# Two-layer graph kernel on one core: the last pass's row statistics and norms shared out anew, adjacency turned by halves, two fetches and one copy at other places

## The chip, the cores and the metric

The kernel runs on 1 core of one Trainium2 chip. The metric is the device time of one execution in microseconds (us). Engines are called PE (TensorE), ACT (ScalarE), DVE (VectorE), POOL (GpSimd) and SP (SyncE, which here only issues DMAs).

## The reference

Eight batches, each with x (1024 rows of 512) and a sparse adj (1024 x 1024). Cut to what matters:

```
x = layernorm(x + L0(x, adj))
x = layernorm(x + L1(x, adj))

L0: w = exp(-0.5 * (adj - mean_k)^2 / (1e-14 + precision_k^2))   for 4 kernels k
    w = w / sum_k w;  ws_k = row sum of w_k
    out[:, k-th 128 columns] = ws_k * x @ W_k.T
L1: top1 = argmax(mean over rows of x @ router_w + router_b)       one of 4 experts per batch
    out = adj @ (x @ expert_w[top1])
    y = relu(batchnorm of out over all batches of one expert)
```

## The kernel before

A tile is 128 rows of one batch: 64 tiles, 8 per batch. Products are made of fp16 halves (high and low part, three products for one). One loop of steps n runs over the tiles on every engine; the engines keep in step by semaphores alone, and each engine's order is as written.

**Main loop, step n.** SP loads adj tile n+2 (L342) and x tile n+3 (L350), turns adj tile n+1 (L362, a transposing DMA from `adj_cut` into `adjT`) and x tile n+2 (L369), stores finished pairs of x1 rows (L459) and L1 units (L487). POOL scales and splits adj tile n+1 (L526 to L531) and x tile n+2 (L538, L540), squares a part (L546, L549), and in odd steps norms two finished tiles (`norm_pair`, L556 to L575). `adj_in` is a ring of 3 tiles. ACT makes squares and exponentials of tile n (L677, L683, L689) and the reciprocal of the sum for tile n-1 as Ln and Exp (L693, L695); DVE adds the four weights up in `ps_t` (L1000), makes weighted row sums (L962), adds the product to x (L984) and takes statistics (L933, L939). PE multiplies x by W (L1156, bank `ps_h`), then the L1 units.

**L1 units.** L1 is computed in the order adj @ x first, then times the expert. A z unit u (8 per batch) is a 128 x 512 block of the transposed adj @ x: 24 matmuls into one of two `ps_z` banks (L1170). ACT copies its high part to `zT` (`take_z`, L705), DVE its low part (`low_z`, L927). PE may start unit u only when the low part of unit u-2 is done. Units 0 to 3 of a batch use the first half of adj's rows, 4 to 7 the second. Unit n-9 is made in step n; step 11 alone makes two, 1 and 2. Four z units later, o unit u multiplies `zT` by the batch's expert `w_sel` (L1188) in step u+13. The expert is picked by a small chain on DVE that ends in `hot_row` (L921) in step 8m+12 for batch m; SP waits for it (L475), and then fetches 1 MB to `w_sel` (L476) in step 8m+13, ahead of that step's turned tiles.

**`adjT`** is double-buffered by batch, laid out as (batch parity, high or low, tile, row): both halves of the rows lie mixed, so its space comes free only when all 8 z units of the batch are done.

**After the loop** come the remaining z and o units on PE, then the batchnorm constants, and the last pass over n = 0 to 7 (batches 7, 6, 0, 1, ..., 5). For each n: L1 output `o` and x1 come back from DRAM into space that the main loop left (`fetch_o`, `fetch_x1`); `affine` applies the constants (ACT L781, POOL L637 for n = 2 and 5); PE transposes each 128 x 512 row tile back (L1237); DVE adds relu of it to x1 (L1110 plain, L1113 with a row sum). "Even" rows get their statistics on DVE (bn_stats L1088, bn_aggr L1096), the others, "odd" rows, get their row sum with the addition and their squares on ACT (L790). ACT turns both into 1/std (L810, L813), and POOL norms the 8 row tiles (L629); for n = 6 ACT norms the last four (L796), with mean times 1/std from POOL (L623). SP stores y in halves of 1 MB (L417), the last one in two pieces (L409, L411).

Even rows are every second one, and all of the last four. ACT's written order in the last pass (L850 ff.) is: half of `affine(n+1)`, `odd_squares(n-2, 1)`, `inverse_std(n-2)`, the other half, `odd_squares(n-1, 0)`.

Of the kernel before, what the change touches and what calls it, by code (L numbers as in the profile page):

```python
# [12 lines left out]
P = 128  # L13
# [39 lines left out]
def gnn_program(nc, x, adj, mean_rel, prec_rel, w0, router_w, router_b, expert_w, gamma, beta, x1_spill,  # L53
# [15 lines left out]
    with ExitStack() as ctx:  # L69
# [11 lines left out]
        adjT = sb("adjT", [P, 2, 2, T, NR], F16)  # L81
# [99 lines left out]
        adjT_flat = flat(adjT[:], "a h t n").bitcast(F32)  # L181
# [52 lines left out]
        early_in = flat(adjT[:, 1], "h t n").bitcast(F32).rearrange("p (e n) -> p e n", e=E)  # L234
# [26 lines left out]

        def even_rows(j):

            return (j + 1) // 2 if j <= END_ROWS else END_ROWS // 2 + j - END_ROWS

        def is_even(j):
            return j % 2 == 0 or j >= END_ROWS
# [66 lines left out]
        def _(sp):  # L334
# [17 lines left out]
            def turn_adj(m):  # L352

                b, t = m // T, m % T
                if m == T:
                    sp.wait_ge(dve_wlo, 2 * (E - 1))
                if t == 0:
                    wait(sp, pe_z, (b - 2) * T + G)
                if t == G:
                    wait(sp, pe_z, (b - 2) * T + T)  # L360
                sp.wait_ge(pool_al, m + 1)
                sp.dma_start_transpose(adjT[:, b % 2, :, :, t * P:(t + 1) * P].rearrange("p h t n -> p (h t) n"),  # L362
                                       flat(adj_cut[:, m % 2], "h n")).then_inc(adj_turned[m % 2], 16)
# [12 lines left out]
            def fetch_o(n):  # L376
# [7 lines left out]
                elif 1 < n < NB:  # L384
                    if n == 2:
                        sp.wait_ge(pe_h, TILES)
                    elif n == 3:
                        sp.wait_ge(pe_z, TILES - T)
                    elif n == 4:
                        sp.wait_ge(pe_z, TILES)  # L390
                    elif n == 5:
                        sp.wait_ge(pe_o, TILES)
# [8 lines left out]
                    for h in range(2):  # L401
                        sp.dma_start(o_buf[i][h], o_lines[b, h]).then_inc(o_back[i], 16)

            def store_y(n):
                for g in range(2):
                    dst = rows_of(out, n)[g]
                    if n == NB - 1 and g == 1:
                        sp.wait_ge(dve_out, G // 2)
                        sp.dma_start(dst[:, 0:G // 2], y_buf[n][g][:, 0:G // 2]).then_inc(y_stored[n % RING], 16)  # L409
                        sp.wait_ge(act_out, G + G // 2)  # L410
                        sp.dma_start(dst[:, G // 2:G], y_buf[n][g][:, G // 2:G]).then_inc(y_stored[n % RING], 16)  # L411
                        continue
                    if n == NB - 2 and g == 1:
                        sp.wait_ge(act_out, G)
                    else:
                        sp.wait_ge(pool_out, n * T + (g + 1) * G - (G if n == NB - 1 else 0))
# [36 lines left out]
            for n in range(LAST):  # L453
# [10 lines left out]
                if u % T == 0 and 0 <= u < TILES:  # L464
                    m = u // T
# [6 lines left out]
                    wait(sp, pe_o, u)  # L472
                    if u == 0:
                        sp.wait_ge(planes_stored, 16 * E)
# [24 lines left out]
            for n in range(4, RING):  # L499
                fetch_o(n)  # L500
                fetch_x1(n)
# [14 lines left out]
        def _(pool):  # L516
# [93 lines left out]
            def minus_mean(n, first, last):  # L610

                at, even, odd = n % 4, slice(first, last, 2), slice(first + 1, last, 2)
                pool.wait_ge(dve_mv2, even_rows(n * T + last))
                g.tensor_scalar(r_neg[:, at, even], r_mv[:, at, even, 0], -1.0, 1.0, ALU.mult, ALU.mult).then_inc(pool_small, 1)
                pool.wait_ge(dve_y2, n * T + last)
                g.tensor_scalar(r_neg[:, at, odd], r_mv[:, at, odd, 0], -1.0 / D, 1.0, ALU.mult, ALU.mult).then_inc(pool_small, 1)
# [29 lines left out]
            for n in range(NB):  # L646
# [20 lines left out]
        def _(act):  # L667
# [29 lines left out]
            def take_z(n):  # L697
                for u in z_unit(n):
# [25 lines left out]
            for n in range(LAST):  # L724
# [16 lines left out]
                if z_taken_first(n - 1):  # L741
                    take_z(n - 1)
                take_o(n - 1)
                if not z_taken_first(n - 1):
                    take_z(n - 1)
# [38 lines left out]
            def odd_squares(n, h):  # L784

                for t in (h * G + 1, h * G + 3):
                    k = n * G + t // 2
# [10 lines left out]

            lns = [0]

            def inverse_std(n, first, last):

                at = n % 4
                groups = [(slice(first, last), 1.0)]
                if n * T + last <= END_ROWS:
                    groups = [(slice(first, last, 2), 1.0), (slice(first + 1, last, 2), float(D) ** -3)]
                    act.wait_ge(act_ssq, n * G + last // 2)
                act.wait_ge(dve_mv2, even_rows(n * T + last))
                for rows, scale in groups:
                    s.activation(r_lnv[:, at, rows], r_mv[:, at, rows, 1], ACT.Ln, bias=eps_out, scale=scale).then_inc(act_lnv, 1)  # L810
# [8 lines left out]
            for n in range(2, NB + 1):  # L819
# [18 lines left out]
        def _(dve):  # L838
# [290 lines left out]
        def _(pe):  # L1129
# [30 lines left out]
            def z_product(u):  # L1160
# [5 lines left out]
                for t in range(T):  # L1166
                    if u % T == 0:
                        pe.wait_ge(pool_1l, u + t + 1)
                    for i, (left, right) in enumerate(PRODUCTS):
                        last = te.matmul(ps_z[:, u % 2, :], x1p[:, b % 2, left, t, k * P:(k + 1) * P],  # L1170
                                         adjT[:, b % 2, right, t, half * HALF:(half + 1) * HALF],
# [95 lines left out]
```

## Time and profile before

| | us |
|---|---|
| median of 3 runs | 880.13 |
| lowest to highest | 879.94 to 881.65 |
| profiled execution, its own time | 878.73 |
| span in the profile | 876.9 |
| PE, DVE, ACT, POOL busy | 754.6, 754.9, 756.3, 704.8 |

The profile divides one execution into instructions with start and duration. "Idle before <-X" is how long the engine stood still before an instruction, and whose semaphore ended it. The main loop runs to about 710 us, PE alone goes on to 797 us, and the last pass fills the rest.

### The profile page before, as it was taken

Reading aid. Unit: us, or ns where it says so; the run is one execution under the profiler, and the core shown is the slowest. Engines: PE = TensorE matmul, PEld = TensorE weight load, DVE = VectorE, ACT = ScalarE, POOL = GpSimd, SP = SyncE. Lnnn points to the kernel's source line nnn. Section 1 sums busy time; section 2 is a strip of 40 time slices with the busy share of each in tenths; the row PEclk is TensorE's granted clock in tenths of the full one; section 3 lists DMA queues with packets and bytes.
Section 4 is the critical chain, followed back from the end, with each engine's and each line's share of the span. In section 5 each row is a group of like instructions: output and inputs, shape, how many; then the busy total and the mean of one; then the engine's idle time right before and its main releaser. Section 6 shows DMA issues by size and latency. Waiting matters only on the chain.

```text
span 876.9 us, 12591 instructions
## 1 busy us (share of the span) xinstructions
PE 754.6 (86%) x3922; PEld 356.6 (41%) x3922; DVE 754.9 (86%) x1643; ACT 756.3 (86%) x774; POOL 704.8 (80%) x808
## 2 busy tenths in 40 slices
PE   1444469899999999999999999999999999997772
PEld 1111124344444444444444444444444444444561
DVE  2999988999999999999999999999999992226995
ACT  6999998999999999999999999999999961115983
POOL 6599989899999999999999999999999732003795
PEclk9766669999999999999999999999999999998996
DMA  8899998988797779888987797779887828219999
GB/s 231 209 278 260 213 238 190 217 195 193 193 240 193 193 193 240 193 193 193 239 195 193 193 241 192 193 187 242 197 193 168 158 81 339 96 67 397 342 388 390
DMA packets 251254, 191.72 MB, mean 219 GB/s; under 512 B 210098, under 2 KB 210098, under 8 KB 245170
## 3 DMA queue, kind: packets, MB, share of 16 engines
q1 hardware_dynamic: 251042, 190.90, 81.3%
q8 instruction: 31, 0.51, 0.3%
q14 instruction: 37, 0.30, 0.1%
q10 hardware_dynamic: 144, 0.00, 0.0%
HBM read 91.78 MB, written 48.76 MB: 160 GB/s over the span
## 4 chain that ended last, share of the span: by engine, by line
POOL 35%; DVE 28%; PE 15%; ACT 13%; issue 6%; DMA 2%; SPq 1%; POOLq 0%; DVEq 0%; ACTq 0%
DVE ps_t L1000 12%; DVE wgt L962 11%; PE ps_z L1170 8%; POOL adj_cut L531 7%; POOL x_turn L540 4%; POOL adj_cut L529 4%; POOL adj_in L526 3%; POOL x1p L575 3%; PE ps_o L1188 3%; ACT ps_t L689 3%; ACT ps_t L695 3%; ACT ps_t L693 3%; DVE x_in L984 2%; POOL x_in L566 2%; POOL x_turn L538 2%
## 5 line engine op out<-in xcount | busy, mean ns | idle before, releaser
L1170 PE MATMUL ps_z<-adjT,x1p 128*128 128x512 f16 x1536 | 342.3, 379 | 0.6 <-POOL x1p L575 0.6
L1156 PE MATMUL ps_h<-w0T,x_turn 128*128 128x512 f16 x768 | 194.5, 407 | 74.2 <-DVE x_in L984 63.0
L1000 DVE TENSOR_TENSOR ps_t<-ps_t,wgt 128x1024 f32<-128x1024 f32 x192 | 235.4, 1226 | 16.6 <-ACT ps_t L689 11.7
L962 DVE SCALAR_TENSOR_TENSOR wgt<-wgt,ps_t 128x1024 f32<-128x1024 f32 x192 | 224.7, 1215 | 16.4 <-ACT ps_t L695 16.4
L1170 PEld LDWEIGHTS ps_z<-adjT,x1p 128*128 128x128 f16 x1536 | 150.1, 98 | 182.5 <-POOL x1p L575 2.5
L677 ACT ACTIVATE wgt<-adj_in,neg_mu 128x1024 f32<-128x1024 f32 x192 | 205.7, 1135 | 7.3 <-POOL neg_mu L593 7.3
L683 ACT ACTIVATE wgt<-wgt 128x3072 f32<-128x3072 f32 x64 | 176.5, 2758 | 0.0
L1188 PE MATMUL ps_o<-zT,w_sel 128*128 128x512 f16 x696 | 159.7, 379 | 1.7 <-DMA w_sel<-w_planes 0.9
L1156 PEld LDWEIGHTS ps_h<-w0T,x_turn 128*128 128x128 f16 x768 | 74.9, 103 | 182.4 <-issue 103.2
L531 POOL TENSOR_TENSOR adj_cut<-adj_in,adj_cut 128x1024 f16<-128x1024 f32 x64 | 138.3, 2160 | 5.3
L1188 PEld LDWEIGHTS ps_o<-zT,w_sel 128*128 128x128 f16 x696 | 68.0, 98 | 84.2 <-DMA w_sel<-w_planes 1.4
L984 DVE SCALAR_TENSOR_TENSOR x_in<-ps_h,wsum,x_in 128x128 f32<-128x128 f32 x256 | 82.8, 345 | 8.8
L927 DVE SCALAR_TENSOR_TENSOR zT<-ps_z,zT 128x512 f16<-128x512 f32 x64 | 43.3, 676 | 47.7 <-ACT zT L705 47.7
L526 POOL TENSOR_SCALAR adj_in<-adj_in 128x1024 f32<-128x1024 f32 x63 | 66.8, 1061 | 17.0 <-DMA adj_in<-in_adj_dram 12.1
L575 POOL TENSOR_TENSOR x1p<-x_in,x1p 128x512 f16<-128x512 f32 x64 | 75.3, 1177 | 5.3
L540 POOL TENSOR_TENSOR x_turn<-x_in,x_turn 128x512 f16<-128x512 f32 x64 | 74.3, 1161 | 5.3
L689 ACT ACTIVATE ps_t<-adj_in 128x1024 f32<-128x1024 f32 x64 | 65.8, 1028 | 11.0 <-DVE wgt L962 8.7
L529 POOL TENSOR_SCALAR adj_cut<-adj_in 128x1024 f16<-128x1024 f32 x64 | 69.0, 1077 | 5.2
L705 ACT ACTIVATE zT<-ps_z 128x512 f16<-128x512 f32 x64 | 37.3, 584 | 40.1 <-PE ps_z L1170 40.1
L693 ACT ACTIVATE ps_t<-ps_t 128x1024 f32<-128x1024 f32 x64 | 64.6, 1009 | 5.7 <-DVE ps_t L1000 3.5
L695 ACT ACTIVATE ps_t<-ps_t 128x1024 f32<-128x1024 f32 x64 | 64.5, 1008 | 2.0
L677 ACT ACTIVATE adj_in<-adj_in,neg_mu 128x768 f32<-128x768 f32 (+1 forms) x64 | 62.1, 970 | 0.0
(222 smaller groups left out, 810.2 us busy)
## 6 DMA issues: line engine op xcount, KB each, us to landing
adj_in<-in_adj_dram SPq DMA_DIRECT2D x64, 512.0 KB, 4.3
x_in<-in_x_dram SPq DMA_DIRECT2D x64, 256.0 KB, 4.4
x_spill<-x_in SPq DMA_DIRECT2D x28, 512.0 KB, 3.4
out_spill<-o_stage SPq DMA_DIRECT2D x50, 256.0 KB, 3.5
w_sel<-w_planes SPq DMA_DIRECT2D x8, 1024.0 KB, 7.8
adjT<-x_spill SPq DMA_DIRECT2D x6, 1024.0 KB, 8.6
out_dram<-adjT SPq DMA_DIRECT2D x5, 1024.0 KB, 6.3
adjT<-out_spill SPq DMA_DIRECT2D x4, 1024.0 KB, 12.6
```

The costliest lines, as they stand in the source:

```text
L529: g.tensor_scalar(cut[:, 0, :], tile, 1.0, 1.0, ALU.mult, ALU.mult).then_inc(pool_ah, 1)
L531: g.tensor_tensor(cut[:, 1, :], tile, cut[:, 0, :], ALU.subtract).then_inc(pool_al, 1)
L540: g.tensor_tensor(cut[:, 1, :], tile, cut[:, 0, :], ALU.subtract).then_inc(pool_xl, 1)
L575: g.tensor_tensor(x1p[:, b % 2, 1, t, :], row, x1p[:, b % 2, 0, t, :], ALU.subtract).then_inc(pool_1l, 1)
L677: s.activation(to, adj_in[:, n % ADJ_RING, first:NR], ACT.Square, bias=neg_mu[:, k:k + 1], scale=spread[k]).then_inc(act_sq, 1)
L683: s.activation(w, w, ACT.Exp, scale=-1.0).then_inc(act_w, 1)
L962: v.scalar_tensor_tensor(out=wgt[:, m % 2, j, :], in0=wgt[:, m % 2, j, :], scalar=SUM_SCALE / W0_SCALE, in1=tot, op0=ALU.mult, op1=ALU.mul ...
L984: last = v.scalar_tensor_tensor(out=row[:, f], in0=ps_h[:, m % 2, f], scalar=wsum[:, m % 2, COLUMN[k]:COLUMN[k] + 1], in1=row[:, f], op0=A ...
L1000: v.tensor_tensor(tot, tot, wgt[:, n % 2, j, :], ALU.add).then_inc(dve_tot, 1)
L1156: last = te.matmul(ps_h[:, n % 2, :], xT[:, n % 2, left, c, :], w0T[:, right, c, :], start=(c + i == 0), stop=(c == C - 1 and i == 2))
L1170: last = te.matmul(ps_z[:, u % 2, :], x1p[:, b % 2, left, t, k * P:(k + 1) * P], adjT[:, b % 2, right, t, half * HALF:(half + 1) * HALF], ...
L1188: last = te.matmul(ps_out(u), w_sel[:, left, c, k * P:(k + 1) * P], zT[:, right, half, c, :], start=(c + i == 0), stop=(c == C - 1 and i = ...
```

## The change

1. **Rows of n = 5 and 6** (`few`): one row tile in four is even (was one in two). The squares of four more row tiles go from DVE's bn_stats to ACT.
2. **Norms of n = 5**: as for n = 6, POOL norms four row tiles and ACT the last four (`norm_late`). ACT's norms of n = 5 stand after `odd_squares(6, 0)`.
3. **`adjT` by halves**: laid out as (batch parity, half, high or low, tile, row within the half). Parts 4 and 5 of the buffer, the place of `o` for n = 4, are now the first half of the last batch, and come free after z unit 59 instead of 63. `fetch_o(4)` moves into `fetch_x1(3)`; the first half of `fetch_o(5)` waits for z unit 63 instead of the last o unit.
4. **Expert's fetch**: in step 8m+12 instead of 8m+13, ahead of that step's turned tiles.
5. **Z unit 2**: ACT's copy goes behind `weigh_others(12)`, DVE's low part from step 12 to the start of step 13.

```diff
-        adjT = sb("adjT", [P, 2, 2, T, NR], F16)
+        adjT = sb("adjT", [P, 2, 2, 2, T, HALF], F16)
...
+        def few(n):
+            return n in (5, 6)
+        def is_even(j):
+            return j % (4 if few(j // T) else 2) == 0 or j >= END_ROWS
...
+        def z_halves(n):
+            return z_unit(n)[:1], z_unit(n)[1:]
...
                     elif n == 4:
+                        sp.wait_ge(pe_z, TILES - G)
+                    elif n == 5:
                         sp.wait_ge(pe_z, TILES)
-                    elif n == 5:
-                        sp.wait_ge(pe_o, TILES)
...
                     for h in range(2):
+                        if n == 5 and h == 1:
+                            sp.wait_ge(pe_o, TILES)
                         sp.dma_start(o_buf[i][h], o_lines[b, h]).then_inc(o_back[i], 16)
...
                     if n == 3 and g == 1:
+                        fetch_o(4)
                         sp.wait_ge(pe_z, TILES)
...
-                if u % T == 0 and 0 <= u < TILES:
-                    m = u // T
+                if (u + 1) % T == 0 and 0 <= u + 1 < TILES:
+                    m = (u + 1) // T
...
                     sp.wait_ge(dve_route, m + 1)
-                    wait(sp, pe_o, u)
+                    wait(sp, pe_o, u + 1)
...
-                    if n == NB - 2:
+                    if few(n):
                         minus_mean_over_std(n, G, T)
-                    norm_rows(n, range(0, G if n == NB - 2 else T))
+                    norm_rows(n, range(0, G if few(n) else T))
...
                     weigh_others(n)
+                    take_z(z_halves(n - 1)[1])
...
                 if n == NB:
-                    act.wait_ge(pool_nmr, 1)
-                    norm(NB - 2, range(G, T))
+                    norm_late(NB - 2)
                 odd_squares(n - 1, 0)
+                if n == NB - 1:
+                    norm_late(NB - 3)
...
-                    for u in z_unit(n - 1):
+                    for u in (*z_halves(n - 2)[1], *z_halves(n - 1)[0]):
                         low_z(u)
```

How the instructions stand before and after, at three places. The lines of the changed kernel have other numbers; the operations are the same.

ACT from the z copies of step 12 on, before (L705 copies a z unit, L693 and L695 make the reciprocal, L683 the exponentials, L677 the squares):

```order
L705 ACTIVATE zT<-ps_z 128x512 x2
L693 ACTIVATE ps_t<-ps_t 128x1024
L695 ACTIVATE ps_t<-ps_t 128x1024
L683 ACTIVATE wgt<-wgt 128x3072
L677 ACTIVATE adj_in<-adj_in,neg_mu 128x1024
L689 ACTIVATE ps_t<-adj_in 128x1024
```

The same place in the changed kernel:

```order
L727 ACTIVATE zT<-ps_z 128x512
L715 ACTIVATE ps_t<-ps_t 128x1024
L717 ACTIVATE ps_t<-ps_t 128x1024
L705 ACTIVATE wgt<-wgt 128x3072
L727 ACTIVATE zT<-ps_z 128x512
L699 ACTIVATE adj_in<-adj_in,neg_mu 128x1024
L711 ACTIVATE ps_t<-adj_in 128x1024
```

The second copy, of unit 2, now stands behind the reciprocal and the exponentials.

SP in steps 20 and 21, before (the row of `w_sel` is the fetch of batch 1's expert, TENSOR_LOAD the read of its number):

```order
L362 DMA_TRANSPOSE adjT<-adj_cut 128x16x128
L487 DMA out_spill<-o_stage 128x512
L369 DMA_TRANSPOSE x_turn<-x_turn 128x8x128
L342 DMA adj_in<-in_adj_dram 128x1024
L350 DMA x_in<-in_x_dram 128x512
L475 TENSOR_LOAD sc_int
L475 ISA x2
L476 ISA
L476 DMA w_sel<-w_planes 128x4096
L362 DMA_TRANSPOSE adjT<-adj_cut 128x16x128
```

In the changed kernel:

```order
L494 TENSOR_LOAD sc_int
L494 ISA x2
L495 ISA
L495 DMA w_sel<-w_planes 128x4096
L378 DMA_TRANSPOSE adjT<-adj_cut 128x16x128
L506 DMA out_spill<-o_stage 128x512
L385 DMA_TRANSPOSE x_turn<-x_turn 128x8x128
L358 DMA adj_in<-in_adj_dram 128x1024
L366 DMA x_in<-in_x_dram 128x512
L378 DMA_TRANSPOSE adjT<-adj_cut 128x16x128
```

The wait for the expert's number and the fetch moved ahead of a turned adj tile, a store, a turned x tile and the loads of adj tile 23 and x tile 24.

ACT in the last pass, before, from the squares of n = 5 (in `zT`) on; n = 6 lies in `x_turn` and `w0T`, n = 7 in `adjT`:

```order
L790 ACTIVATE ps_z,adj_in<-zT,adj_in 128x512 x4
L810 ACTIVATE adj_in<-adj_in,eps 128x4 x2
L813 ACTIVATE adj_in<-adj_in 128x8
L790 ACTIVATE ps_z,adj_in<-x_turn,adj_in 128x512 x2
L790 ACTIVATE ps_z,adj_in<-w0T,adj_in 128x512 x2
L810 ACTIVATE adj_in<-adj_in,eps 128x4 x2
L813 ACTIVATE adj_in<-adj_in 128x8
L796 ACTIVATE w0T<-w0T,adj_in 128x512 x4
L790 ACTIVATE ps_z,adj_in<-adjT,adj_in 128x512 x2
```

In the changed kernel:

```order
L815 ACTIVATE ps_z,adj_in<-zT,adj_in 128x512 x6
L841 ACTIVATE adj_in<-adj_in,eps 128x2
L841 ACTIVATE adj_in<-adj_in,eps 128x2x3
L844 ACTIVATE adj_in<-adj_in 128x8
L815 ACTIVATE ps_z,adj_in<-x_turn,adj_in 128x512 x3
L821 ACTIVATE zT<-zT,adj_in 128x512 x4
L815 ACTIVATE ps_z,adj_in<-w0T,adj_in 128x512 x3
L841 ACTIVATE adj_in<-adj_in,eps 128x2
L841 ACTIVATE adj_in<-adj_in,eps 128x2x3
L844 ACTIVATE adj_in<-adj_in 128x8
L821 ACTIVATE w0T<-w0T,adj_in 128x512 x4
L815 ACTIVATE ps_z,adj_in<-adjT,adj_in 128x512 x2
```

ACT has four more squares and four more norms here, and the norms of n = 5 stand between the two groups of squares of n = 6.

## Rows read from the trace of the kernel before

**Rows 1.** Waits from 160 to 720 us: total us, times, longest us

```profile
POOL adj_in L546 <- ACT wgt L677: 6.6, 1, 6.6
ACT ps_t L689 <- POOL adj_in L549: 1.8, 7, 0.3
PE ps_o L1188 <- DMA w_sel<-w_planes: 0.9, 1, 0.9
```

**Rows 2.** Timeline of ACT, step 12: start us, duration us, operation, idle before

```profile
146.55 0.60 ACT L705 ACTIVATE zT<-ps_z 128x512 f16<-128x512 f32 x1 [2.21 <-PE ps_z L1170]
147.04 1.02 ACT L693 ACTIVATE ps_t<-ps_t 128x1024 f32<-128x1024 f32 x1
```

**Rows 3.** Timeline of DVE, steps 12 and 13

```profile
143.60 1.23 DVE L1000 TENSOR_TENSOR ps_t<-ps_t,wgt 128x1024 f32<-128x1024 f32 x1
...
154.02 1.22 DVE L1000 TENSOR_TENSOR ps_t<-ps_t,wgt 128x1024 f32<-128x1024 f32 x1
...
158.53 0.67 DVE L927 SCALAR_TENSOR_TENSOR zT<-ps_z,zT 128x512 f16<-128x512 f32 x1
159.13 0.17 DVE L939 BATCH_NORM_AGGREGATE y_mv<-y_stat 128x2 f32<-128x6 f32 x1
```

**Rows 4.** Timeline of POOL, steps 13 and 22

```profile
159.46 0.19 POOL L556 TENSOR_SCALAR rstd<-y_mv 128x2 f32<-128x2 f32 x1 [3.04 <-DVE y_mv L939]
...
253.80 1.05 POOL L526 TENSOR_SCALAR adj_in<-adj_in 128x1024 f32<-128x1024 f32 x1
```

**Rows 5.** Timeline of DVE, step 20: the expert's number is ready

```profile
241.15 0.20 DVE L921 TENSOR_SCALAR hot_row<-ps_s,sc_idx 1x4 f32<-1x4 f32 x1
```

**Rows 6.** Timeline of SP's queue, steps 21 and 22

```profile
242.85 0.35 SPq L476 DMA_DIRECT2D w_sel<-w_planes  x1
243.89 6.42 SPq L362 DMA_TRANSPOSE adjT<-adj_cut  x1
...
253.00 0.48 SPq L342 DMA_DIRECT2D adj_in<-in_adj_dram  x1
```

**Rows 7.** DMA issues of the whole page: count, KB each, median us to landing

```profile
adj_in<-in_adj_dram SPq DMA_DIRECT2D x64, 512.0 KB, 4.3
...
w_sel<-w_planes SPq DMA_DIRECT2D x8, 1024.0 KB, 7.8
```

**Rows 8.** DMA issues from 752 to 760 us alone, same columns

```profile
w_sel<-w_planes SPq DMA_DIRECT2D x1, 1024.0 KB, 4.8
```

**Rows 9.** Windows: busy us of PE, PEld, DVE, ACT, POOL; clock, DMA share, GB/s

```profile
765.00:775.00 10.00, 10.00 (x48) 4.51 (x46) 5.29 (x25) 1.79 (x3) 0.00 (x0) 1.00 0.00 1
...
846.00:862.00 16.00, 11.29 (x64) 8.94 (x64) 16.00 (x53) 9.24 (x26) 15.71 (x28) 0.99 1.01 402
```

**Rows 10.** Timeline of DVE, last pass, n = 7

```profile
857.97 0.69 DVE L1088 BATCH_NORM_STATS2 y_stat<-adjT 128x6 f32<-128x512 f32 x1
858.57 0.67 DVE L1110 SCALAR_TENSOR_TENSOR adjT<-ps_h,adjT 128x512 f32<-128x512 f32 x1
```

**Rows 11.** Timeline of ACT, last pass, n = 5 to 7

```profile
846.01 0.67 ACT L790 ACTIVATE ps_z<-zT,adj_in 128x512 f32<-128x512 f32 x1
...
846.72 0.67 ACT L790 ACTIVATE ps_z<-zT,adj_in 128x512 f32<-128x512 f32 x1
...
850.56 0.21 ACT L813 ACTIVATE adj_in<-adj_in 128x8 f32<-128x8 f32 x1
...
858.09 0.21 ACT L813 ACTIVATE adj_in<-adj_in 128x8 f32<-128x8 f32 x1
860.36 2.93 ACT L796 ACTIVATE w0T<-w0T,adj_in 128x512 f32<-128x512 f32 x4 [2.07 <-POOL adj_in L623]
...
864.51 0.18 ACT L790 ACTIVATION_READ_ACCUMULATOR ps_z<-adjT,adj_in 128x1 f32 x1
...
865.25 0.21 ACT L813 ACTIVATE adj_in<-adj_in 128x4 f32<-128x4 f32 x1
```

**Rows 12.** Timeline of POOL, last pass, n = 5 to 7

```profile
853.67 6.05 POOL L629 TENSOR_SCALAR zT<-zT,adj_in 128x512 f32<-128x512 f32 x8
...
860.12 0.20 POOL L623 TENSOR_TENSOR adj_in<-adj_in 128x4 f32<-128x4 f32 x1
860.31 3.03 POOL L629 TENSOR_SCALAR x_turn<-x_turn,adj_in 128x512 f32<-128x512 f32 x4
...
865.63 3.47 POOL L629 TENSOR_SCALAR adjT<-adjT,adj_in 128x512 f32<-128x512 f32 x4 [1.97 <-ACT adj_in L813]
```

**Rows 13.** Timeline of SP's queue: the first of the last three stores

```profile
869.12 0.33 SPq L417 DMA_DIRECT2D out_dram<-adjT  x1
```

More of the change, by code:

```diff
@@ L180, in gnn_program @@
         wgt_flat = flat(wgt[:], "a k n")
-        adjT_flat = flat(adjT[:], "a h t n").bitcast(F32)
+        adjT_flat = flat(adjT[:], "a g h t n").bitcast(F32)
         x1p_flat = flat(x1p[:], "a h t n").bitcast(F32)
@@ L260, in gnn_program, with of_rows @@
         END_ROWS = NB * T - G
+        def few(n):
+            return n in (5, 6)
+        def is_even(j):
+            return j % (4 if few(j // T) else 2) == 0 or j >= END_ROWS
         def even_rows(j):
-            return (j + 1) // 2 if j <= END_ROWS else END_ROWS // 2 + j - END_ROWS
-        def is_even(j):
-            return j % 2 == 0 or j >= END_ROWS
+            return sum(is_even(i) for i in range(j))
+        def of_rows(x, n, first, last, odd):
+            if not few(n):
+                return x[:, slice(first + odd, last, 2)]
+            lines = x[:, first:last].rearrange("p (h t) -> p h t", t=G)
+            return lines[:, :, slice(1, G) if odd else slice(0, 1)]
         BY_POOL = (2, 5)
@@ L498, in _ @@
             fetch_x1(3)
-            for n in range(4, RING):
-                fetch_o(n)
-                fetch_x1(n)
+            fetch_x1(4)
+            fetch_o(5)
+            fetch_x1(5)
             fetch_o(6)
@@ L695, in sum_reciprocal, with take_z @@
                 s.activation(tot, tot, ACT.Exp, scale=-1.0).then_inc(act_rec, 1)
-            def take_z(n):
-                for u in z_unit(n):
+            def take_z(units):
+                for u in units:
                     half, k = u % T // G, u % G
@@ L784, in odd_squares @@
             def odd_squares(n, h):
-                for t in (h * G + 1, h * G + 3):
-                    k = n * G + t // 2
+                for t in range(h * G, (h + 1) * G):
+                    if is_even(n * T + t):
+                        continue
+                    k = n * T + t - even_rows(n * T + t)
                     act.wait_ge(dve_y2, n * T + t + 1)
@@ L797, in norm, with norm_late @@
                                  scale=r_std[:, n % 4, t:t + 1]).then_inc(act_out, 1)
+            def norm_late(n):
+                act.wait_ge(pool_nmr, sum(few(m) for m in range(n + 1)))
+                norm(n, range(G, T))
             lns = [0]
@@ L803, in inverse_std @@
                 at = n % 4
-                groups = [(slice(first, last), 1.0)]
+                lnv, square = r_lnv[:, at], r_mv[:, at, :, 1]
+                groups = [(lnv[:, first:last], square[:, first:last], 1.0)]
                 if n * T + last <= END_ROWS:
-                    groups = [(slice(first, last, 2), 1.0), (slice(first + 1, last, 2), float(D) ** -3)]
-                    act.wait_ge(act_ssq, n * G + last // 2)
+                    groups = [(of_rows(lnv, n, first, last, odd), of_rows(square, n, first, last, odd), scale)
+                              for odd, scale in ((0, 1.0), (1, float(D) ** -3))]
+                    act.wait_ge(act_ssq, n * T + last - even_rows(n * T + last))
                 act.wait_ge(dve_mv2, even_rows(n * T + last))
-                for rows, scale in groups:
-                    s.activation(r_lnv[:, at, rows], r_mv[:, at, rows, 1], ACT.Ln, bias=eps_out, scale=scale).then_inc(act_lnv, 1)
+                for to, of, scale in groups:
+                    s.activation(to, of, ACT.Ln, bias=eps_out, scale=scale).then_inc(act_lnv, 1)
                 lns[0] += len(groups)
@@ L1170, in z_product @@
                         last = te.matmul(ps_z[:, u % 2, :], x1p[:, b % 2, left, t, k * P:(k + 1) * P],
-                                         adjT[:, b % 2, right, t, half * HALF:(half + 1) * HALF],
+                                         adjT[:, b % 2, half, right, t, :],
                                          start=(t + i == 0), stop=(t == T - 1 and i == 2))
```

27 lines of the change are left out of this document (15 added, 12 removed).

## The prediction

> **What bounds the kernel now.** I read the waits of the main loop first, then the timelines of ACT, DVE and POOL where a wait stands out, then the last pass by windows and by each engine's timeline.
>
> Main loop: from 160 to 720 us POOL waits for nothing worth naming but once for 6.6 us, at the very end where it has no more tiles [rows 1]. An engine that never waits sets the pace. ACT and DVE form a ring of nearly the same length: ACT waits for POOL's square seven times, 1.8 us in all [rows 1]. So whatever lets POOL start its unbroken run earlier moves the whole loop and, behind it, the products that PE makes alone up to 797 us. That run starts at 159.46, after a wait of 3.04 us for DVE's statistics [rows 4].
>
> Last pass: DVE is busy 16.00 of 16 us and POOL 15.71, while DMA stands at 1.01 of its share and ACT works only 9.24 [rows 9]. Three resources are full at once; ACT has the room. The end goes by POOL: it norms n = 5 from 853.67, hands out L623 at 860.12 [rows 12], ACT, which had 1/std ready at 858.30 and stood idle 2.07 us, norms its rows till 863.3, then squares rows of n = 7 and gives 1/std at 865.46 [rows 11]; POOL norms four rows from 865.63 to 869.10, and SP's first store of the last three goes out at 869.12 [rows 12, 13].
>
> **Z unit 2's copy (step 12).** ACT waits 2.21 us for PE before it copies unit 2, and the reciprocal behind it starts at 147.04 [rows 2]. Without that copy it needs only DVE's sum, which ends at 143.60 + 1.23 = 144.83 [rows 3]: start 144.87, 2.17 us earlier. The copy comes back behind the exponentials, where unit 2 is long done, and takes about 0.5 us of ACT (0.60 less the overlap of two neighbours: 146.55 to 147.04 [rows 2]). So the sum that DVE starts at 154.02 [rows 3] starts 1.7 us earlier, and from there the ACT and DVE ring is 1.7 us ahead. In step 13 DVE has one more low part before its statistics, 0.60 us (158.53 to 159.13 [rows 3]); they come 1.7 - 0.6 = 1.1 us earlier, and so does POOL's start at 159.46 [rows 4]. The ring's extra 0.6 us is lost, since it waits for POOL after some steps.
>
> One item adds to this. PE waits once for `w_sel`, 0.9 us [rows 1]; ACT then falls back some 0.5 us behind POOL and stays there. With a fetch that lands earlier this goes. So the loop ends between 1.1 (POOL's shift alone) and 1.7 us (all of the ring's) earlier; I take 1.5.
>
> **The expert's fetch.** For m = 1 the number is ready at 241.15 + 0.20 = 241.35 [rows 5], and SP issues the fetch at 242.85 [rows 6], held up by two loads ahead of it. Now SP stands waiting, and issues at about 242.1. What is queued behind it counts: turned tile 21, a store, turned x tile 22, then the load of adj tile 23, which POOL wants at 253.80 [rows 4]. In the trace the turned tile behind the fetch holds SP for 6.42 us [rows 6]: its end, 250.31, is 0.3 us before the fetch lands by the median of 7.8 us. A fetch with nothing ahead of it in the queues lands in 4.8 us [rows 8]. By that: 242.1 + 4.8 - 0.3 = 246.6 for the turned tile. From the end of the turned tile to the adj load are 253.00 - 250.31 = 2.7 us [rows 6], of which a store of x1 (0.6) now falls behind it: load at 248.7, landed 4.3 us later [rows 7] at 253.0. POOL wants it at 253.80, in later batches some 0.6 us later against the number, once ACT and DVE run right behind POOL. Margin 0.8 to 1.4 us: cost nothing. With the median 7.8 us it is the first rival. Turned x tile 22 is issued at about 247.4 and wanted by PE only after 255.
>
> The Trainium skill (DMA: Bandwidth & Descriptors, Anatomy of one DMA) gives 2.0 us plus bytes over 436 GB/s, for another way of issuing: 4.4 us for 1 MB, near the 4.8 that the trace has for a fetch alone, against the 7.8 with loads ahead of it. By it the margin would be 0.4 us wider and the sum the same.
>
> **adjT by halves, fetches of the last pass.** DMA stands still in 765 to 775 us (share 0.00 [rows 9]), so 2 MB of n = 4 move from the crowded time after 784 to the idle time after 755. PE reads the same 512 columns in one piece as before, and the transposing DMA writes pieces of the same 128 columns at another distance: I cost that at nothing, between plus and minus 1 us. At 1 MB in 2.5 us (425 GB/s) the move frees 4.9 us of DMA. But no engine of the last pass waits for a fetch now; the gain comes at the end alone, where the stores of n = 6 still run when those of n = 7 are issued at 869.12. The last 2 MB need 4.9 us in any case, and the end at 876.9 leaves 7.8 us from the issue; a start at once and a late completion take some 7.3. So 0.3 to 0.8 us, I take 0.5.
>
> **Statistics and norms.** DVE loses four bn_stats, 0.60 us each (857.97 to 858.57 [rows 10]), and four aggregates of about 0.1: 2.7 us, and the rows of n = 7 are ready 2.7 us earlier. This does not reach the end, because ACT now becomes the bound. ACT, in times of the old trace: six squares of n = 5, 0.71 apart (846.01 to 846.72 [rows 11]), till 850.3; 1/std ready at 851.1 (before 850.77); three squares of n = 6 till 853.2. POOL ends n = 4 and hands out L623 for n = 5 at 853.8, by the same 0.45 us that it takes behind n = 5 [rows 12]. ACT norms four rows, 4 x 0.71, till 856.7; three more squares till 858.9; 1/std of n = 6 at 859.7, where it was 858.30. POOL, with four rows less, has waited since 857 and gives L623 at 860.0 (before 860.32). ACT's norms end at 862.9, two squares at 864.4 (before 864.69), 1/std at 865.15 (before 865.46). POOL's last four rows and the store move by the same 0.3 us. So of DVE's 2.7 us and POOL's 3 us, 0.3 are left. Bounds: 0.3 later if each of the eight more ACT operations costs 0.1 more, 2.7 earlier if ACT were no bound.
>
> **Sum.** 1.5 + 0.5 + 0.3 = 2.3 us. The profiled execution took 878.73 (span 876.9): 876.4. Its time lies 1.4 below the median of 880.13, so the median becomes **877.8**.
>
> **Rivals.**
> 1. *The fetch holds SP, and POOL runs dry.* If the fetch takes 7.8 us [rows 7] with nothing ahead of it, the turned tile ends at 249.6, adj tile 23 lands at 256.0, and POOL, which has no slack, waits 1.5 to 2.2 us after each of seven fetches: 10 to 15 us. The point from which it decides is a landing of about 6 us. For it: the four queued items are all ahead of the load now. Against it: the 4.8 us row. Net 880.1 - 2.3 + 12 = 889, slower by 1%.
> 2. *ACT is no bound in the last pass* (it fits its new work into its idle time): DVE's 2.7 us count, and the freed DMA time lets them: 880.1 - 1.5 - 0.5 - 2.7 = 875.4. Against it: ACT's list above has no idle stretch longer than 0.6 us between 846 and 857.
> 3. *The main loop gives nothing back*: PE or a DMA takes the place of the wait at 146.55. PE has to make units 3 and 4 in the same order, and unit 4 needs unit 2's low part just when PE is ready for it (157.5 against 157.9). Then only the last pass's 0.8 us are left: 879.3, within 0.2%. The same holds if the turned halves or ACT's new work cost as much as they give.
>
> **How the numbers follow.** Forecast 0.52, rival 3 and its kin 0.24, rival 2 0.12, rival 1 0.12. A measurement of this kernel can tell some 0.2% from no change, 1.76 us: faster means below 878.4, slower above 881.9. The forecast, with main loop 1.1 to 1.7, end 0.3 to 0.8, statistics -0.3 to 0.6, runs from 877.0 to 879.0; about a tenth of its chance lies in "same". Faster 0.6, same 0.28, slower 0.12. The range leaves out rival 1 and little else: 875.0 to 881.0.
>
> **What would show it.** Step 12: no wait of ACT before unit 2's copy, POOL's L556 of step 13 about 1.1 us earlier. Main loop: POOL without waits at tile 8m+15, ACT waiting for L549 oftener than seven times. From 755 us a fetch of 2 MB. Last pass: ACT full from 846 to 864, POOL idle some 2.5 us between its norms of n = 5 and n = 6, DVE waiting or ending early; last stores issued about 1.8 us earlier. Wrong would be: waits of POOL for `adj_in` with the fetch ahead (rival 1), or POOL's last norms 2 us or more earlier than 0.3 against 797 us (rival 2).

## The result, and the profile after

| | before | after |
|---|---|---|
| median, us | 880.17 (879.49 to 881.78, 8 runs) | **883.67** (883.3 to 885.45, 8 runs) |
| profiled execution, its own time | 878.73 | 883.32 |
| span in the profile | 876.9 | 881.5 |

The ratio is 1.0038, 95% interval 1.0028 to 1.0047: slower by 0.4%. Forecast were 877.8 us and a range of 875.0 to 881.0. On another chip, in the experiments below, the same kernel came to 885.06 us against 879.91 (1.0057, 1.0043 to 1.0071).

The waits of after from 160 to 720 us (total us, times, longest us) answer to [rows 1]:

```profile
ACT ps_t L711 <- POOL adj_in L568: 10.6, 24, 1.6
...
POOL adj_in L565 <- ACT wgt L699: 5.9, 1, 5.9
POOL adj_in L545 <- DMA adj_in<-in_adj_dram: 5.6, 8, 1.4
```

The last row is new. POOL, which sets the pace of the loop and had not waited for an adj tile, now waits for one after each of the first seven fetches of an expert (the eighth has no adj tile behind it). ACT, one step behind in the ring, hands this on: 10.6 us in 24 waits where it had 1.8 in 7. PE's one wait for `w_sel` [rows 1] is gone, as meant.

SP's own waits of after over the same stretch, same columns, say what it stands for (L50 is the helper that waits on a semaphore, here for PE's o unit 8m-1; L494 reads the expert's number):

```profile
SPq L50 <- PE ps_o L1220: 39.1, 6, 7.6
SPq L494 <- DVE hot_row L953: 16.1, 6, 2.7
```

That is 55 us in six fetches, 9 us each. Before, SP waited for neither of the two. Most of the time, 39.1 us, goes to o unit 8m-1, which still reads the old expert in `w_sel`; the expert's number ends the last 2.7 us. About half of the 9 us SP would have stood in any case: before, it stood until 236.33 (below) for POOL's part of tile 21. The other half is new, and while SP stands, nothing else is issued. In the window of 238 to 242 us (columns as in [rows 9]; the first line is before, the second after) DMA was full, and is empty now:

```profile
238.00:242.00 4.00, 4.00 (x20) 1.85 (x19) 3.87 (x14) 3.71 (x4) 3.67 (x6) 1.00 1.10 234
```

```profile
238.00:242.00 4.00, 4.00 (x20) 1.80 (x19) 3.87 (x13) 3.70 (x5) 3.67 (x5) 1.00 0.00 0
```

SP's queue before, steps 20 and 21, which goes on in [rows 6] (start us, us that SP is held, operation):

```profile
236.33 1.48 SPq L362 DMA_TRANSPOSE adjT<-adj_cut  x1
...
241.20 0.33 SPq L342 DMA_DIRECT2D adj_in<-in_adj_dram  x1
```

The same of after, steps 20 to 22, behind DVE's line that gives the expert's number (ready at 240.39):

```profile
240.19 0.20 DVE L953 TENSOR_SCALAR hot_row<-ps_s,sc_idx 1x4 f32<-1x4 f32 x1
```

```profile
241.16 0.35 SPq L495 DMA_DIRECT2D w_sel<-w_planes  x1
241.56 5.26 SPq L378 DMA_TRANSPOSE adjT<-adj_cut  x1
246.87 0.57 SPq L506 DMA_DIRECT2D out_spill<-o_stage  x1
247.55 1.29 SPq L385 DMA_TRANSPOSE x_turn<-x_turn  x1
248.88 0.58 SPq L358 DMA_DIRECT2D adj_in<-in_adj_dram  x1
249.56 0.38 SPq L366 DMA_DIRECT2D x_in<-in_x_dram  x1
249.98 3.77 SPq L378 DMA_TRANSPOSE adjT<-adj_cut  x1
...
256.44 1.47 SPq L358 DMA_DIRECT2D adj_in<-in_adj_dram  x1
```

The first load (tile 23) goes out at 248.88, 7.7 us later than before (241.20), and just makes it: its data lands 4.4 us later, and POOL wants it at 253.51. From here to the second load (tile 24) SP never stands and makes up 4.2 of the 7.7 us, but not the rest: turned tile 22 between the two holds it for 3.77 us, and the load goes out at 256.44 instead of 253.00 [rows 6]. It takes 5.1 us to land, and POOL runs dry:

```profile
261.57 1.05 POOL L545 TENSOR_SCALAR adj_in<-adj_in 128x1024 f32<-128x1024 f32 x1 [0.59 <-DMA adj_in<-in_adj_dram]
```

There are eight such waits, of 0.3 to 1.4 us: at the second load behind the fetch (tiles 24, 32, 40, 48, 56) and, at tiles 15, 39 and 63, at the first one. The first ACT instruction behind the products (`e_lnv`) started at 799.48 us before and starts at 803.10 now: the loop has lost 3.6 us. The last pass adds nothing of that size. Its first row came 4.44 us behind `e_lnv` in both; the first of the last three stores is issued 69.34 us behind it, 69.64 before, and the span ends 78.42 us behind it, 77.45 before.

Such a place in one trace is good to about 2 us only. The two lines below are the exponentials of step 11, in the kernel before and in the one with the fetch alone (see the experiments), which up to there are the same program. In seven kernels that are the same up to there this instruction starts between 135.86 and 138.16 us.

```profile
135.86 2.76 ACT L683 ACTIVATE wgt<-wgt 128x3072 f32<-128x3072 f32 x1
```

```profile
138.10 2.76 ACT L683 ACTIVATE wgt<-wgt 128x3072 f32<-128x3072 f32 x1
```

So below, "counted from step 11" is the time from this instruction to `e_lnv`: 663.6 us before, 666.7 in the changed kernel, a loss of 3.1 us.

Step 12 did what it should. ACT's timeline of after answers to [rows 2]: the wait of 2.21 us for PE is gone, and the second copy has moved behind the exponentials.

```profile
144.34 0.57 ACT L727 ACTIVATE zT<-ps_z 128x512 f16<-128x512 f32 x1
145.43 1.01 ACT L715 ACTIVATE ps_t<-ps_t 128x1024 f32<-128x1024 f32 x1 [0.52 <-DVE ps_t L1032]
...
147.39 2.75 ACT L705 ACTIVATE wgt<-wgt 128x3072 f32<-128x3072 f32 x1
150.05 0.59 ACT L727 ACTIVATE zT<-ps_z 128x512 f16<-128x512 f32 x1
```

The windows of after answer to [rows 9]. The fetch of n = 4 did move to 755 to 765 us (DMA share 0.44 before), and in the last pass ACT is full where it had room:

```profile
755.00:765.00 10.00, 10.00 (x48) 4.52 (x46) 1.32 (x5) 0.60 (x1) 0.00 (x0) 1.00 0.74 294
...
846.00:862.00 16.00, 13.41 (x80) 11.10 (x80) 16.00 (x51) 15.21 (x37) 14.62 (x25) 1.00 1.01 381
```

### The profile page after: what moved, and what is told of

Read it like the earlier page. It is cut to its first block, busy times and chain, and to the rows that moved or that the text cites. A ratio compares the mean times of both kernels' runs of the same rounds, so it can differ in the third digit from the quotient of the medians.

```text
span 881.5 us, 12592 instructions
## 1 busy us (share of the span) xinstructions
PE 754.3 (86%) x3922; PEld 355.8 (40%) x3922; DVE 753.4 (85%) x1635; ACT 761.3 (86%) x786; POOL 701.8 (80%) x805
## 4 chain that ended last, share of the span: by engine, by line
POOL 66%; PE 12%; issue 7%; DVE 7%; ACT 7%; DMA 1%; POOLq 0%; DVEq 0%; ACTq 0%
POOL adj_cut L550 13%; POOL x_turn L559 7%; POOL x1p L594 7%; POOL adj_cut L548 7%; POOL adj_in L545 7%; PE ps_z L1202 6%; POOL x_in L585 5%; POOL x_turn L557 4%; POOL x1p L592 4%; DVE ps_t L1032 3%; POOL adj_in L568 3%; POOL adj_in L565 3%; PE ps_o L1220 3%; POOL rstd L578 2%; PE ps_t L1220 2%
## 5 line engine op out<-in xcount | busy, mean ns | idle before, releaser
L705 ACT ACTIVATE wgt<-wgt 128x3072 f32<-128x3072 f32 x64 | 176.5, 2757 | 0.0
L711 ACT ACTIVATE ps_t<-adj_in 128x1024 f32<-128x1024 f32 x64 | 65.8, 1028 | 17.0 <-POOL adj_in L568 10.6
```

What stands on the lines that cost most here:

```text
L705: s.activation(w, w, ACT.Exp, scale=-1.0).then_inc(act_w, 1)
```

## Experiments

Theory A after the two traces: the fetch's new place is the loss, because SP stands there with a turned tile and the next loads behind it; the other parts give the 1 to 2 us that were forecast. Rivals: the halved layout slows turned tiles or products; the bytes of the fetch ahead of the loads are the cost, wherever SP waits; a part of the loss lies in the last pass.

### The fetch put back

```
-                if (u + 1) % T == 0 and 0 <= u + 1 < TILES:
-                    m = (u + 1) // T
+                if u % T == 0 and 0 <= u < TILES:
+                    m = u // T
...
-                    wait(sp, pe_o, u + 1)
-                    if m == 0:
+                    wait(sp, pe_o, u)
+                    if u == 0:
```

> The changed kernel with the expert's fetch put back to step 8m+13, all else as changed. Theory A (the fetch a step up is the whole loss): POOL no longer waits for adj_in, the first ACT instruction behind the products (e_lnv, 799.44 us before, 803.08 after) comes at 797.7 to 798.5 us, and the median is 877.5 to 879.0 us, faster than before by 1 to 2.5. Theory B (adjT by halves slows the transposing DMAs or the products, and the fetch only fell in with it): the median stays above 882 us and e_lnv above 801. Theory C (part of the loss sits in the last pass, where DMA is full from 835 us on): e_lnv as in A, but the median not under 879.5.

Measured: 878.12 us against 879.53, ratio 0.9986 (0.9977 to 0.9995). `e_lnv` at 798.10, 2.7 us earlier than before counted from step 11. POOL no longer waits for `adj_in`. With that one part undone the change is a gain of 1.4 us. Theories B and C fall. The fetch's place is worth some 5.5 us here by the medians (883.67 and 878.12, taken on two occasions), 4.6 us by the two ratios.

### The fetch alone

The same lines the other way round, in the kernel before.

> The kernel before with one thing changed: the expert's fetch is issued in step 8m+12, behind the two loads and ahead of the turned tile, instead of 8m+13. Theory A: POOL waits 0.3 to 1.5 us for adj_in after each of seven fetches, 4.5 to 6 us in all, PE's one wait for w_sel goes, and the median is 883.5 to 885.5 us. Theory B: POOL waits less than 1 us in all and the median stays at 879.3 to 880.5.

Measured: 888.05 us, ratio 1.0091 (1.0075 to 1.0107). The sign and the mechanism are as expected, the size is 2.6 us beyond my range. A part of the extra lies behind the very first fetch: tiles 15 and 16 cost 1.13 and 0.56 (0.40 and none in after). POOL's timeline of this run:

```profile
169.39 1.05 POOL L526 TENSOR_SCALAR adj_in<-adj_in 128x1024 f32<-128x1024 f32 x1 [1.13 <-DMA adj_in<-in_adj_dram]
177.42 1.05 POOL L526 TENSOR_SCALAR adj_in<-adj_in 128x1024 f32<-128x1024 f32 x1 [0.56 <-DMA adj_in<-in_adj_dram]
```

Counted from step 11 this trace loses 6.5 us.

### The copy alone

```
                 if n < TILES:
                     weigh_others(n)
+                    take_z(z_halves(n - 1)[1])
```

with `take_z` of the first part alone at the old place, and DVE's low part of unit 2 one step later.

> The kernel before with one thing changed: z unit 2 is copied by ACT behind the exponentials of step 12, and its low part is made by DVE one step later. Theory A (the ring of ACT, DVE and POOL keeps what step 12 gives): POOL's and ACT's work of the loop 1.1 to 1.7 us earlier, median 878.4 to 879.2. Rival (what is won in step 12 is lost at the next wait, PE or POOL takes its place): shift under 0.5 us by tile 24, median 879.8 to 880.3.

Measured: 877.71 us against 879.53, ratio 0.9983 (0.9974 to 0.9992), a gain of 1.8 us. `e_lnv` at 797.17, 2.3 us earlier (2.7 counted from step 11). The rival falls: nothing took the place of the wait. The trace says where it comes from. POOL's L556 of step 13 starts 14.55 us behind ACT's copy of unit 1, where it was 15.69 (144.16 and 158.71, before 143.77 and 159.46): 1.1 us, as forecast. The other 1.6 us come in the stretch behind it, where POOL waits for nothing and its operations are a little shorter; that is not shown to be the copy's doing, see the last section. This kernel has the lowest median of those that store the whole output, below the one before and the changed one; by ratio (0.9983) it can't be told from two others below (0.9986 with the fetch back, 0.9984 with copy and late fetch).

### The halves alone

`adjT` by halves and the early fetch of n = 4, in the kernel before.

> The kernel before with adjT laid out by halves and the fetch of n = 4 (2 MB) moved ahead of the end of the z products, nothing else. Theory A: the main loop is where it was (e_lnv at 799.2 to 799.7 us), DMA moves 2 MB around 757 to 764 us and then idles as much at 796 to 820, since what follows waits for buffers, and the median is 879.7 to 880.5. Rival B (the halves slow each turned tile or the products): e_lnv 1 us or more later. Rival D (what I predicted: the moved 2 MB free DMA for the end): 0.3 to 0.8 us earlier, 879.4 to 879.9.

Measured: 879.68 against 879.53, ratio 0.9996 (0.9987 to 1.0005). The windows of this run:

```profile
755.00:765.00 10.00, 10.00 (x48) 4.56 (x47) 0.69 (x1) 1.55 (x3) 0.00 (x0) 1.00 0.98 408
797.00:820.00 23.00, 14.73 (x84) 12.17 (x81) 20.64 (x67) 19.07 (x35) 14.52 (x20) 0.85 0.78 284
```

The kernel before has DMA at 0.44 and 0.93 of its share there. The 2 MB did move into the idle time, and DMA idles more from 797 to 820 instead: what comes next in SP's order waits for space that the last pass itself must free. Neither a loss nor a gain is seen, though the interval of the median (-1.1 to +0.4 us) has room for the forecast's 0.5. (`e_lnv` came at 799.96, 0.3 us later than I had set as the bound; counted from step 11 it is where it was, 663.6 us.)

### The last pass alone

The new sharing of statistics and norms, in the kernel before.

> The kernel before with only the last pass's statistics and norms shared anew (four rows of n = 5 normed by ACT, three of four rows of n = 5 and 6 squared by ACT). Theory A' (DMA is full from 20 us behind e_lnv to the end, and has the same 21.9 MB to move): last three stores issued 0.2 to 0.5 us earlier against e_lnv, but the end 77.2 to 78.2 us behind e_lnv (before 77.44), median 879.3 to 880.3. Rival (what I predicted: the 0.3 us reach the end): end 76.9 to 77.2 behind e_lnv, median about 879.2.

Measured: 880.33 against 880.41, ratio 1.000 (0.9991 to 1.0009). The first of the last three stores is issued 69.21 us behind `e_lnv` (69.64 before), the span ends 77.96 us behind it (77.45). The 0.4 us at the issue are not seen at the end. That fits Theory A'; it doesn't exclude the forecast's 0.3 us, since the ends of the traces here differ by up to 1.2 us among themselves and the median's interval is 0.8 us to either side.

### Fetch and copy together

> The kernel before with the fetch a step up and unit 2's copy moved, nothing else. The fetch alone cost 8.5 us, on top of the other parts 5.5. Theory I (the two interact: part of the 8.5 us is lost in steps 12 to 15, where ACT's wait for unit 2 stands too): median 882.5 to 884.5, the same as the changed kernel. Rival (no interaction, 8.5 - 1.8): 886.2, and then parts of the last pass or the halves would have to give 2.5 us.

Measured: 886.96 against 880.41, ratio 1.0078 (1.0061 to 1.0096), single runs from 884.26 to 890.15. My range for Theory I is missed: the whole interval lies above it. Against the fetch alone the copy gives 2.0 us by the medians (8.5 less 6.5), as it does alone, but the two intervals overlap, they are from two chips, and counted from step 11 the traces lose 6.9 us here and 6.5 there. Whether the two interact is not shown either way. In this profile POOL waits for `adj_in` 10.8 us in 10 waits from 185 to 720 us, in that of after 5.2 us in 7. So the price of the fetch's place isn't a fixed number; the changed kernel without its last pass, below, takes that up.

### The fetch earlier, but with nothing behind SP's wait

The changed kernel with the whole block (wait and fetch) moved behind `turn_x(n + 2)` of the same step 8m+12, so ahead of the next step's loads.

> The changed kernel with the fetch issued at the end of step 8m+12: behind the turned adj tile, the store and the turned x tile, ahead of the next step's loads. Theory A (the loss comes from what stands behind SP's wait): for m = 1 the turned tile is out at 236 to 239 us, SP waits some 1 us at most, the fetch goes out at 241.4, the adj load of tile 23 at about 242 and lands by 250, before POOL wants it at 253; no wait of POOL for adj_in in the loop, none of PE for w_sel; median 877.0 to 878.3. Rival (the fetch's bytes ahead of the loads are what starves POOL, wherever SP waits): POOL waits for adj_in in three batches or more, median above 879.5.

Measured: 879.15 against 880.41, ratio 0.9989 (0.998 to 0.9997). SP's queue of this run:

```profile
236.22 1.48 SPq L378 DMA_TRANSPOSE adjT<-adj_cut  x1
...
241.94 0.36 SPq L508 DMA_DIRECT2D w_sel<-w_planes  x1
242.35 0.42 SPq L358 DMA_DIRECT2D adj_in<-in_adj_dram  x1
242.88 0.37 SPq L366 DMA_DIRECT2D x_in<-in_x_dram  x1
243.78 5.48 SPq L378 DMA_TRANSPOSE adjT<-adj_cut  x1
...
252.10 0.48 SPq L358 DMA_DIRECT2D adj_in<-in_adj_dram  x1
```

The fetch goes out 0.9 us earlier than before [rows 6], with its 1 MB ahead of both loads, and the second load is even 0.9 us earlier than before. Over 160 to 720 us SP now waits for the expert's number once, for 0.2 us, and for the o unit not at all, where it had stood 55 us. POOL never waits for `adj_in`, PE never for `w_sel`. The rival (the bytes ahead of the loads starve POOL) falls. Against the fetch at its old place (ratio 0.9986) nothing is gained, since POOL sets the pace and had no use for it. My 877.0 to 878.3 was too low by 0.9 us; as much lies between the two chips, for the kernel before came to 879.53 on the one from which I had my numbers and to 880.41 on this one. The same move in the kernel with the copy alone:

> The kernel before with two things changed: unit 2's copy moved, and the fetch at the end of step 8m+12 as in the kernel above; last pass and adjT as before. Theory A: against the copy alone (877.7) PE's one wait for w_sel goes (0.8 us) and ACT keeps closer to POOL: 876.8 to 877.8. Rival (the same as above): above 879.5.

Measured: 878.78 against 880.41, ratio 0.9984 (0.9975 to 0.9993), the same gain as the copy alone (0.9983); the median itself lies 1 us above what I expected, again the difference of the two chips.

### SP's wait alone

```
+                if (u + 1) % T == 0 and 0 <= u + 1 < TILES:
+                    sp.wait_ge(dve_route, (u + 1) // T + 1)
+                    wait(sp, pe_o, u + 1)
                 if u % T == 0 and 0 <= u < TILES:
                     m = u // T
```

in the kernel with the copy alone.

> The kernel with the copy moved (877.7 us) and nothing else but two waits: in step 8m+12, behind the two loads and ahead of the turned tile, SP waits for the expert's number and for o unit 8m-1; the fetch itself stays in step 8m+13. No byte moves another way, only SP stands. Theory A (what costs is what stands behind SP's wait, whatever is fetched there): POOL waits for adj_in behind five batches or more, 3 to 10 us in all, median 882 to 887. Rival (the fetch's 1 MB ahead of the turned tile and the loads is what costs): POOL does not wait, median 877.3 to 878.7.

Measured: **930.77** against 879.91, ratio 1.0599 (1.0571 to 1.0627). The rival falls, and Theory A's direction holds by far more than its size. The waits of this run from 160 to 720 us:

```profile
PEld ps_o L1196 <- DMA w_sel<-w_planes: 24.7, 7, 4.7
ACT o_stage L729 <- PE ps_o L1196: 23.8, 6, 6.5
PE ps_o L1196 <- DMA w_sel<-w_planes: 21.3, 7, 4.2
...
POOL adj_in L533 <- DMA adj_in<-in_adj_dram: 10.5, 5, 2.9
```

SP's queue of this run:

```profile
243.08 1.48 SPq L366 DMA_TRANSPOSE adjT<-adj_cut  x1
...
247.34 0.83 SPq L346 DMA_DIRECT2D adj_in<-in_adj_dram  x1
...
249.50 0.35 SPq L483 DMA_DIRECT2D w_sel<-w_planes  x1
249.91 6.41 SPq L366 DMA_TRANSPOSE adjT<-adj_cut  x1
```

POOL's waits for `adj_in` (10.5 us) are a little over what I had expected of it. What I had missed is that the wait holds the fetch back too: it goes out at 249.50, 6.4 us after the number (before: 1.5), and PE needs it, seven times, 21.3 us in all. PE then also loses clock: after the wait of 2.65 us that ends at 256.57 the granted clock of 256 to 261 us is 0.66 (1.00 is 2.4 GHz; the stretch is in part at the lower level, 1.2 GHz), and the 12 products of the o unit take 4.43 us; they took 2.76 behind two of the seven waits and 4.2 to 4.9 behind the others. How the 51 us add up from these and the waits that they hand on was not followed. What the run shows is that SP's standing alone, with no byte more, starves POOL, and that it costs far more where the fetch doesn't come early in return.

### The changed kernel without its last pass, and again as it is

> The changed kernel without the new sharing of the last pass: fetch a step up, copy moved, adjT by halves. Without the halves the same came to 887.0 us, and the changed kernel to 883.7. Theory H (the halves make the turned tiles behind the fetch cheaper): POOL's waits for adj_in 4 to 6 us, median 883 to 884.5. Rival I (loads and POOL's demand lie within 1 us of each other seven times, and small shifts decide each time; the layout has no part of its own): anything from 882 to 888, with single runs spread over 3 us or more, and turned tiles behind the fetch as long with the halves as without, 3.5 to 4.8 us.

> The changed kernel itself once more, so that it stands beside the others of this call on one chip. Theory A asks for 882.5 to 885.5 us, with POOL waiting 4 to 8 us for adj_in; by rival I above its single runs spread over 3 us, and the profiled one need not show the same sum of waits (5.6 us) as the first.

Measured: 885.62 (1.0061, 1.0047 to 1.0075) and 885.06 (1.0057, 1.0043 to 1.0071) against 879.91. The last pass's part makes no difference that can be told: 0.6 us, with intervals of 1.2 us to either side. POOL waits for `adj_in` 6.4 us in 10 waits and 8.1 us in 8; the first profile of the changed kernel had 5.6 in 8. The turned tiles 8m+14, the first behind two fresh loads, hold SP for 3.5 to 4.1 us in the profile of after and 3.5 to 4.4 in those of the two kernels with the fetch a step up and the old layout: no more apart than their own scatter. Between 887.0 (no halves) and 885.6 (halves), measured on different chips, I can't tell an effect of the layout from scatter. But it may be there: counted from step 11 the three traces with halves and early fetch lose 2.8, 3.1 and 4.1 us, the two without halves 6.5 and 6.9. With the fetch at its old place no cost of the halves shows. Whether they make the early fetch cheaper stays open.

### One store less

The changed kernel with the fetch back, without the 2 MB of stores of n = 4.

> The changed kernel with the fetch put back to step 8m+13 (878.1 us), and the two stores of n = 4 (2 MB of the output) left out, so that DMA has 2 MB less to move before the last stores; no engine but SP does anything else. Theory T (DMA, full from 20 us behind e_lnv on, has about 1 MB queued when the last three stores are issued): the end comes 1.5 to 2.5 us earlier, 875.6 to 876.6, and the last issue is where it was, 69.2 us behind e_lnv. Rival (the end hangs on the issue of the last store alone): 877.8 to 878.4.

Measured: 876.96 against 879.91, ratio 0.996 (0.9946 to 0.9974); with the stores it had been 0.9986, on another chip. The first of the last three stores is issued 69.29 us behind `e_lnv` (69.19 with the stores), the end comes 76.21 behind it (78.12): 1.9 us earlier with the issue unchanged. Theory T holds: at the end DMA has a backlog, and the end follows its bytes and not the last issue alone.

## Why the prediction was wrong

**What bounds the kernel: right.** POOL sets the pace of the loop, and whatever shifts it shifts the end. That is just why a small wait in front of it cost what it did.

**Copy of unit 2: right.** Forecast 1.1 to 1.7 us for the main loop, measured alone 1.8 (0.7 to 2.3 by the interval). ACT's steps came as worked out, and so did POOL's start, by 1.1 us. That the rest of the loop gave as much again is luck, as far as the traces tell: POOL's shorter operations, which two kernels without the copy have too. The 1.5 that I took also held something for PE's wait for `w_sel`; the kernels without that wait are no faster for it.

**The expert's fetch: this step failed.** The step is "Margin 0.8 to 1.4 us: cost nothing"; it cost 4.6 to 8.5 us. The working followed SP's queue from the fetch to the load of tile 23 and stopped there. Up to there it looks close: fetch at 241.16 (forecast 242.1), turned tile out by 246.8 (246.6), load at 248.88 (248.7). That is luck in part: the number itself came 1.0 us earlier in this trace (240.39, before 241.35), and counted from it the load is 1.1 us later than forecast. The fetch had been priced at 4.8 us by the single row from 752 us on [rows 8] and landed in 5.8. Four terms were wrong or missing.
- The landing, 5.8 and not 4.8 us, took most of the margin at tile 23: 0.2 us of it was left.
- The load behind that one, of tile 24, was never looked at. It goes out 3.4 us later than before, since SP has made up only 4.2 of the 7.7 us by which the load ahead of it is late. POOL waits for the tile at this place in five of six batches.
- The margin of 0.8 to 1.4 us was taken from one place (tile 23) and a median landing of 4.3 us. The two loads landed in 4.4 and 5.1 us, and at tiles 15, 39 and 63 the first load was late too.
- SP's standing was priced by its end alone. It's a hole of some 9 us of SP's time per batch, 5 of them taken from a turned tile that went at 236.33 before. What it bought was a fetch 1.7 us earlier for PE, which had waited once, for 0.9 us.

Rival 1 named this mechanism ("the fetch holds SP, and POOL runs dry") with a chance of 0.12 and 10 to 15 us. Its point of decision, a landing of about 6 us, was the wrong one: the fetch landed in 5.8 us by the median, not 7.8, and POOL ran dry all the same, in smaller pieces of 0.3 to 1.4 us. Since "no wait" and "late by 2 us" were the only two cases, the 4 to 8 us between them had no chance at all.

**Fetch of n = 4: moved as said, no gain seen.** Forecast 0.5 us, of which the 7.3 us for "a start at once and a late completion" had no row. The space in the queue was given back before 820 us, as the halves alone show; their interval (-1.1 to +0.4 us) is too wide to exclude the 0.5.

**Statistics and norms: right at the issue, not seen at the end.** Forecast 0.3 us at the last stores. In the five kernels with this part they are issued 69.19 to 69.37 us behind `e_lnv`, in the eight others (before among them, the one without the stores of n = 4 not counted) 69.43 to 69.65. But the end, 77.4 to 78.6 us behind `e_lnv` in all thirteen, doesn't visibly follow it. ACT was the bound of the issue, as forecast (15.21 of 16 us), and rival 2 didn't come. DMA's backlog has a hand in the end, as the 1.9 us for one pair of stores less show.

**Sum.** Forecast were -1.5 (loop), 0 (fetch), -0.5 (end) and -0.3 (statistics). By the kernels that do one part alone or leave one out it was -1.8 for the copy, +4.6 to +8.5 for the fetch (4.6 by ratios against the changed kernel, 8.5 alone), 0 for the halves with the early fetch of n = 4 (-1.1 to +0.4 by the interval), 0 for the last pass (0.8 to either side); the changed kernel itself stands at +3.5 on the first chip and +5.2 on another.

## What to carry to other kernels

A queue that issues DMAs in order is an engine: a wait moved to an earlier place in it must be priced as a stretch in which everything behind it stands, and followed until the queue is back where it was, not only to the first transfer of interest. If a fetch has to wait for a late number, put it behind all that is ready, and ahead of what is not yet wanted. And where the pacing engine has no slack, a margin has to be checked for every transfer it consumes, with the longest landing in the trace and not the median.

## What the chip showed beside

**How long a turned tile holds SP depends on what is queued ahead.** The same transposing DMA of an adj tile held it for 1.48 us with the DMA engines at 0.25 of their share (236.22, the kernel with the fetch at the end of the step), 3.77 us behind two loads of 0.75 MB together, 5.26 us behind the 1 MB fetch, 5.48 us behind the fetch and the two loads, and 6.42 us [rows 6] behind the same in another order, the two loads first. From batch to batch the last case takes 5.7 to 8.2 us. I had taken the 6.42 us for the fetch alone.

**A load's landing is longer than its bytes.** The 512 KB loads landed in 4.3 us by the median and in 5.1 us at the place that decided. The Trainium skill (DMA: Bandwidth & Descriptors, Anatomy of one DMA) gives 2.0 us plus bytes over 436 GB/s, for DMAs that GpSimd issues, so 3.2 us as an estimate; the trace, with DMAs issued by SP and others under way, is 1.1 to 1.9 us above it.

**A full DMA share isn't a full rate.** Two windows of the kernel before, both all but full:

```profile
843.00:845.00 2.00, 1.55 (x10) 1.19 (x9) 2.00 (x7) 1.94 (x6) 2.00 (x4) 1.00 0.96 270
852.00:856.00 4.00, 3.01 (x19) 2.47 (x19) 4.00 (x13) 1.63 (x4) 3.90 (x8) 1.00 1.01 420
```

In the first one the fetches of x1 run beside stores, in the second stores run alone. Why the mix is slower wasn't tried.

**POOL's pace differs by 0.2% between kernels in which it never waits.** The norm of x1 rows from 300 to 590 us, before, with the copy alone, and with the fetch at the end of the step (count, busy us, mean ns of one):

```profile
L566 POOL TENSOR_SCALAR x_in<-x_in,neg_mean,rstd 128x512 f32<-128x512 f32 x26 | 20.1, 774 | 1.4
```

```profile
L570 POOL TENSOR_SCALAR x_in<-x_in,neg_mean,rstd 128x512 f32<-128x512 f32 x26 | 19.9, 767 | 1.4
```

```profile
L585 POOL TENSOR_SCALAR x_in<-x_in,neg_mean,rstd 128x512 f32<-128x512 f32 x26 | 20.1, 772 | 1.4
```

Most of POOL's operations differ likewise, by 1 to 5 ns. Over 14 pairs of tiles that makes 306.36, 305.70 and 306.31 us, some 1.2 us over the loop: nearly the size of the whole gain that was sought. It goes neither with the copy nor with the chip: the kernel with the last pass alone, whose loop is that of before, has 768 ns and 305.8 us, on the chip on which the one with the late fetch had 772 and 306.3. The cause was not tried; I had taken the duration of an operation for fixed.
